# Routing of a mixture of experts, taken batch by batch into the attention of the same layer

## What is computed

```python
x = x + jnp.tanh(g_xattn[2]) * _L2_xattn_ref(_layernorm(x, axis=-1), ctx_512, ctx_512)
x = x + jnp.tanh(g_ffn[2]) * _L2_ffn_ref(_layernorm(x, axis=-1), L2_ffn_router_w, L2_ffn_w1, L2_ffn_w2)
...
logits = xf @ router_w.T
topk_vals, topk_idx = jax.lax.top_k(logits, K)
topk_w = jax.nn.softmax(topk_vals, axis=-1)
...
order = jnp.argsort(exp_id)
x_sorted = xf[order // K]
...
y1 = jax.lax.ragged_dot(x_sorted, jnp.swapaxes(w1, 1, 2), counts)
gate, up = jnp.split(y1, 2, axis=-1)
y_act = jax.nn.silu(gate) * up
y2 = jax.lax.ragged_dot(y_act, jnp.swapaxes(w2, 1, 2), counts)
...
y_pairs = y2[inv] * exp_w[:, None]
y = y_pairs.reshape(T, K, h).sum(axis=1)
```

## Time and profile before

| | us |
|---|---|
| median of 3 runs (4147.03 to 4149.95) | 4148.43 |
| the profiled execution | 4149.84 |
| its span | 4148.0 |
| TensorE busy | 3696.8 (89%) |
| VectorE busy | 1982.5 (48%) |
| ACT busy | 1365.8 (33%) |
| POOL busy | 368.5 (9%) |
| layer 2's attention, from its first score to its last addition | 1142.4 to 1643.5 |
| the tiles' loop begins | 1771.2 |

### The profile page before, as it was taken

The page is one execution under the profiler, slowest core; times in us unless marked ns, Lnnn a source line. Parts: engine busy times, 40 slices in busy tenths (PEclk is TensorE's granted clock), DMA queues, the critical chain, the costliest instruction groups (busy, mean ns, idle before and its releaser), DMA issues.

```text
span 4148.0 us, 35816 instructions
## 1 busy us (share of the span) xinstructions
PE 3696.8 (89%) x11778; PEld 1707.9 (41%) x11779; DVE 1982.5 (48%) x3525; ACT 1365.8 (33%) x2823; POOL 368.5 (9%) x387
## 2 busy tenths in 40 slices
PE   1999999966689998299969999999999998999999
PEld 0444444422344443156633444444444343444443
DVE  8646664153777774211136665656666562111111
ACT  5524341011256666022224343433434341101000
POOL 6000000000222220311110100000000000000000
PEclk6999999978889999599989999999999999999999
DMA  2322212200312330355551100000000001222221
GB/s 114 122 83 98 85 66 66 112 24 0 71 37 49 72 73 13 142 152 162 163 182 55 65 23 34 23 35 35 23 35 23 35 12 66 76 86 86 76 82 55
DMA packets 77384, 291.57 MB, mean 70 GB/s; under 512 B 10424, under 2 KB 11320, under 8 KB 66236
## 3 DMA queue, kind: packets, MB, share of 16 engines
q1 hardware_dynamic: 68928, 264.12, 19.4%
q0 software_dynamic: 8320, 25.71, 2.0%
HBM read 255.68 MB, written 33.59 MB: 70 GB/s over the span
## 4 chain that ended last, share of the span: by engine, by line
PE 78%; DVE 9%; issue 6%; ACT 4%; DMA 1%; POOL 1%; SPq 0%; DVEq 0%; ACTq 0%; POOLq 0%
PE BM L2008 6%; PE BM L2059 5%; PE BM L529 5%; PE BR L529 5%; PE BR L2067 4%; PE BM L364 4%; PE BR L364 4%; PE BS L2043 3%; PE BT L1349 3%; PE BS L545 3%; PE BT L545 3%; PE BM L2018 3%; PE BR L1694 2%; PE BM L1683 2%; PE BR L1683 2%
## 5 line engine op out<-in xcount | busy, mean ns | idle before, releaser
L2119 ACT COPY AR<-BM 128x512 f32<-128x512 f32 x340 | 199.5, 587 | 395.5 <-PE BM L2059 184.5
L2125 ACT ACTIVATE AR<-BS,AR 128x512 f32<-128x512 f32 x256 | 175.7, 690 | 410.1 <-DVE AR L2219 410.1
L2232 DVE SCALAR_TENSOR_TENSOR X<-BR,AR,X 128x512 f32<-128x512 f32 x256 | 191.9, 750 | 211.8 <-PE BR L2067 202.4
L2219 DVE TENSOR_REDUCE AR<-BS 128x2 f32<-128x1024 f32 x128 | 156.9, 1226 | 252.2 <-PE BS L2043 252.2
L2067 PE MATMUL BR<-AR 128*128 128x512 f32 x512 | 254.4, 620 | 3.9 <-DVE X L2232 0.3
L364 PE MATMUL BM<-XT,AR 128*128 (+1 forms) x512 | 233.1, 598 | 4.8 <-DMA AR<-l_w_dram 4.8
L2008 PE MATMUL BM<-XT,AR 128*128 128x512 f32 x512 | 236.6, 605 | 0.7 <-ACT XT L239 0.7
L2059 PE MATMUL BM<-AR 128*128 128x512 f32 x512 | 233.8, 599 | 0.0
L529 PE MATMUL BM<-XT,AR 128*128 128x512 f32 x512 | 230.6, 593 | 0.9 <-ACT AR L632 0.9
L529 PE MATMUL BR<-XT,AR 128*128 128x512 f32 x512 | 230.2, 592 | 0.0
L364 PE MATMUL BR<-XT,AR 128*128 (+1 forms) x512 | 230.2, 592 | 0.0
(11 more groups left out here) (335 smaller groups left out, 5945.2 us busy)
## 6 DMA issues: line engine op xcount, KB each, us to landing
AR<-l_w_dram SPq DMA_DIRECT2D x128, 512.0 KB, 3.5
AR<-l_wq_dram SPq DMA_DIRECT2D x32, 1152.0 KB, 5.1
AR<-l_w_dram SPq DMA_DIRECT2D x42, 768.0 KB, 4.7
AR<-w2h SPq DMA_DIRECT2D x16, 1024.0 KB, 4.7
QS<-qx SPq DMA_DIRECT2D x32, 512.0 KB, 9.4
AR<-l_w_dram SPq DMA_DIRECT2D x16, 1024.0 KB, 4.9
AR<-l_w_dram SPq DMA_DIRECT2D x8, 1408.0 KB, 17.2
made<-AR SPq DMA_DIRECT2D x40, 256.0 KB, 4.8
```

The costliest lines, as they stand in the source:

```text
L2119: nc.scalar.copy(to, BM[:, L3[job] % 2, :]).then_inc(m_free, 1)
L2232: nc.vector.scalar_tensor_tensor(out=xb, in0=BR[:, L3[job] % 2, :], scalar=RS3[:, p % 2, h, st:st + 1], in1=xb, op0=ALU.mult, op1=ALU.add) ...
```

## The change

Batches 0, 1 and 2 are routed while the attention of the next batch runs, and batch 3 alone at the end. With b the batch that is routed, in unit 8(b + 1) + 2 VectorE takes the statistics of the batch just finished; in the unit after it writes XN, TensorE turns it and ACT copies it once; in the next one SP stores the rows to `xnd`, TensorE makes the logits, now with the tokens as weights and the router's 8 columns moving, ACT copies them out, and VectorE chooses the experts; in the next TensorE counts and VectorE works out the places; in the last two POOL scatters, four DMAs each. The normalisation of batch 0 in units 24 and 25 is gone.

So that places are known before all tokens are counted, the table has fixed room, 2048 places for each expert, and is 128 rows of 128. At the end only the rows in use are read: VectorE works out for each partition which row its tile lies in, POOL gathers these rows with an indirect DMA, and TensorE turns them. The token numbers are therefore f32. The places in `made` (YP) are found from the fixed places by taking the room off and adding the start. At the start the table is cleared by four DMAs instead of one. The two copies of turned maxima (MTS) lie on other partitions instead of in other columns, which makes room for the routing's scratch.

```diff
-        ZERO = sb("ZERO", [P, TW], I32)
+        ZERO = sb("ZERO", [P, 32])
...
+        def routed_batch(n, k):
+            return n // KVH - 1 if n >= KVH and n % KVH == k else None
...
+        def store_rows(sp, b):
+            sp.wait_ge(xn_ready, XR[b])
+            sp.dma_start(xnd[b * S:(b + 1) * S, :].rearrange("(s p) d -> p s d", p=P), XN[:, :, :]).then_inc(xnd_in, 16)
+        def route_logits(bank, half):
+            for st in range(ST):
+                for kt in range(KT):
+                    last = nc.tensor.matmul(bank[:, st * E:(st + 1) * E], XT[:, half, kt, st * P:(st + 1) * P], RW[:, kt, :],
+                                            start=kt == 0, stop=kt == KT - 1)
+            return last
+        def route_ranks(bank):
+            n = ST * E
+            ohs = OHS.rearrange("p t e -> p (t e)")
+            nc.tensor.matmul(bank[:, 0:n], TRI, ohs, start=True, stop=True)
+            return nc.tensor.matmul(bank[:, n:2 * n], ONE, ohs, start=True, stop=True)
+        def route_top(v, b, lg):
+            for mx, of, oh in ((MX0, lg, OH0), (MX1, LG2, OH1)):
+                if oh is OH1:
+                    link(v, nc.vector.scalar_tensor_tensor(out=LG2, in0=OH0, scalar=-1.0e30, in1=lg, op0=ALU.mult, op1=ALU.add))
+                link(v, nc.vector.tensor_reduce(mx, of, op=ALU.max, axis=AX.X))
+                link(v, tt(EQ, of, one(mx, E), ALU.is_ge))
+                link(v, tt(EQ, EQ, per_e(PRIO, ST), ALU.mult))
+                link(v, nc.vector.tensor_reduce(MS, EQ, op=ALU.max, axis=AX.X))
+                link(v, tt(oh, EQ, one(MS, E), ALU.is_equal))
+            tt(OHS, OH0, OH1, ALU.add).then_inc(ohs_ready, 1)
+            link(v, tt(EX[:, b * ST:(b + 1) * ST], MX1, MX0, ALU.subtract))
+        def route_rank(v, b, ranks):
+            link(v, nc.vector.tensor_copy(PREF[:, 0, :], PREF[:, ST, :] if b else BASE))
+            for t in range(ST):
+                link(v, tt(PREF[:, t + 1, :], PREF[:, t, :], ranks[:, ST + t, :], ALU.add))
+            link(v, tt(RT[:, 0:ST, :], ranks[:, 0:ST, :], PREF[:, 0:ST, :], ALU.add))
+            for oh, idx in ((OH0, IDX0), (OH1, IDX1)):
+                link(v, tt(EQ, oh, RT[:, 0:ST, :], ALU.mult))
+                link(v, nc.vector.tensor_reduce(POS, EQ, op=ALU.add, axis=AX.X))
+                nc.vector.tensor_copy(idx[:, b * ST:(b + 1) * ST], POS).then_inc(idx_ready, 1)
+                v.wait_ge(idx_ready, 2 * b + (1 if idx is IDX0 else 2))
+        def scatter_tokens(pool, b, j):
+            pool.wait_ge(idx_ready, 2 * b + j + 1)
+            for tile in range(b * ST, (b + 1) * ST):
+                nc.gpsimd.indirect_dma_start(out=table, out_offset=bass.IndirectOffsetOnAxis(ap=(IDX0, IDX1)[j][:, tile:tile + 1], axis=0),
+                                             in_=TOK[:, tile:tile + 1], in_offset=None).then_inc(table_in, 16)
...
@@ l2_tensor @@
+                    if tt == 1 and routed_batch(n, 4) is not None:
+                        logits(routed_batch(n, 4))
+                    if tt == 1 and routed_batch(n, 5) is not None:
+                        ranks(routed_batch(n, 5))
+                    if n % KVH == 1 and tt == 3 and n // KVH < B - 1:
+                        turn_norm("n", n // KVH)
+                    if tt == 3 and routed_batch(n, 3) is not None:
+                        turn_norm("q", routed_batch(n, 3))
...
@@ l2_scalar @@
+            def take_rows(b):
+                for kt in range(KT):
+                    nc.scalar.copy(XT[:, (b + 1) % 2, kt, :], evict(("q", b, kt))).then_inc(e_free, 1)
...
@@ l2_vector @@
+                    if n % KVH == 0 and tt == 3 and b < B - 1:
+                        norm_begin(b + 1)
...
+                    if routed_batch(n, 2) is not None and tt == 3:
+                        v.wait_ge(x_done, 4 * B + b)
+                        norm_begin(b - 1)
+                    if routed_batch(n, 3) is not None and tt == 1:
+                        norm_end(b - 1, ("n", b, KT - 1) if b < B - 1 else ("q", 1, KT - 1), b - 1)
+                    if routed_batch(n, 4) is not None and tt == 3:
+                        v.wait_ge(lg_ready, b)
+                        route_top(v, b - 1, LG)
+                    if routed_batch(n, 5) is not None and tt == 3:
+                        v.wait_ge(rt_ready, b)
+                        route_rank(v, b - 1, RT)
...
@@ l2_pool, at the end of a unit @@
+                if routed_batch(n, 2) is not None:
+                    norm_pool(pool)
+                if routed_batch(n, 6) is not None:
+                    scatter_tokens(pool, routed_batch(n, 6), 0)
+                if routed_batch(n, 7) is not None:
+                    scatter_tokens(pool, routed_batch(n, 7), 1)
...
@@ moe_sync @@
+            for e in range(2):
+                up(e)
+            store_rows(sp, B - 1)
+            for e in range(2, E):
+                up(e)
...
@@ moe_tensor @@
+            norm_tensor(pe)
+            route_logits(start_job(pe, er, r), 0).then_inc(er.full, 1)
+            pe.wait_ge(ohs_ready, B)
+            route_ranks(start_job(pe, er, r)).then_inc(er.full, 1)
+            pe.wait_ge(slt_in, 16)
+            nc.tensor.transpose(start_job(pe, er, r)[:, 0:P], SLT, ID[:, :]).then_inc(er.full, 1)
...
@@ moe_vector @@
+            norm_vector(v, B - 1)
+            route_top(v, B - 1, in_tiles(full(v, er, r), ST))
+            route_rank(v, B - 1, in_tiles(full(v, er, r), 2 * ST))
...
+            nc.vector.tensor_copy(SLOTS, full(v, er, r)[:, 0:TW]).then_inc(slots_ready, 1)
...
@@ moe_pool @@
-            for tile in range(B * ST):
-                for idx in (IDX0, IDX1):
-                    nc.gpsimd.indirect_dma_start(out=table, out_offset=bass.IndirectOffsetOnAxis(ap=idx[:, tile:tile + 1], axis=0),
-                                                 in_=TOK[:, tile:tile + 1], in_offset=None).then_inc(table_in, 16)
-            pool.wait_ge(slots_in, 16)
+            for j in range(2):
+                scatter_tokens(pool, B - 1, j)
+            pool.wait_ge(row_ready, 1)
+            pool.wait_ge(table_in, 2 * B * ST * 16)
+            nc.gpsimd.indirect_dma_start(out=SLT, out_offset=None, in_=table.rearrange("(r n) o -> r (n o)", n=P),
+                                         in_offset=bass.IndirectOffsetOnAxis(ap=ROW, axis=0)).then_inc(slt_in, 16)
+            pool.wait_ge(slots_ready, 1)
```

More of the change, by code:

```diff
@@ L1642, in moe_tensor @@
             pe.wait_ge(x_done, 5 * B)
[L1643 to L1649, removed]
[L1650 to L1660 removed]
+            norm_tensor(pe)
+            pe.wait_ge(turn.free, T_PE.now() + 2)
+            route_logits(start_job(pe, er, r), 0).then_inc(er.full, 1)
[3 more added lines that the diff above has]
+            nc.tensor.transpose(start_job(pe, er, r)[:, 0:P], SLT, ID[:, :]).then_inc(er.full, 1)
             pe.wait_ge(turn.free, T_PE.now() + 2)
@@ L1710, in moe_scalar @@
                 act.sem_inc(q.free, 2)
-            for b in range(B):
-                nc.scalar.copy(LT[0:E, :], full(act, em, m)[0:E, :]).then_inc(em.free, 1)
-                if b < B - 1:
-                    norm_scalar(act, (b + 1) & 1)
+            norm_scalar(act, 0)
             act.wait_ge(pair_exp_in, 1)
@@ L1751, in moe_vector @@
                 v.sem_inc(y_stored[u], 16)
-            v.wait_ge(router_in, 64)
-            nc.vector.memset(ONE, 1.0).then_inc(ones_ready, 1)
-            for b in range(B):
-                bank = full(v, er, r)
-                nc.vector.tensor_copy(LG[:, b * ST:(b + 1) * ST, :], bank[:, 0:ST * E].rearrange("p (s e) -> p s e", e=E)).then_inc(er.free, 1)
-                if b < B - 1:
-                    v.wait_ge(xnd_in, 16 * (b + 1))
-                    norm_vector(v, b + 1)
-                    T_V.step(KT)
@@ L1782, in moe_vector @@
-            bank = full(v, er, r)[:, 0:n128].rearrange("p (t e) -> p t e", e=E)
-            nc.vector.tensor_copy(TOTAL, bank)
-            nc.vector.tensor_copy(SCAN0, bank).then_inc(er.free, 1)
-            v.wait_ge(er.free, r.now() + 2)
+            v.wait_ge(x_done, 5 * B)
+            v.wait_ge(e_full, L2["q", B - 2, KT - 1] + 1)
+            v.wait_ge(xnd_in, 16 * (B - 1))
+            norm_vector(v, B - 1)
+            T_V.step(KT)
+            in_tiles = lambda bank, n: bank[:, 0:n * E].rearrange("p (t e) -> p t e", e=E)
@@ L2317, in _ @@
             sp.wait_ge(zero_ready, 1)
-            sp.dma_start(table.rearrange("(p n) o -> p (n o)", p=P), ZERO[:, :]).then_inc(table_zero, 16)
+            for c in range(4):
+                sp.dma_start(table.rearrange("(p n) o -> p (n o)", p=P)[:, 32 * c:32 * c + 32], ZERO[:, :]).then_inc(table_zero, 16)
             l0_sync(sp)
```

225 lines of the change are left out of this document (127 added, 98 removed).

## The result

The changed kernel takes 4126.67 us (median of four executions, 4124.98 to 4127.68), the kernel before 4148.76 us beside it: ratio 0.9947, 95% interval 0.9932 to 0.9962. It is faster by 22 us, where 48 were forecast, and lies just above the range (4084 to 4126). The span of its profiled execution is 4124.4 us.

The account below looks back on a forecast made before the run. TensorE, busy 89%, gains only where it stands still: the 127.7 us serial chain after layer 2's attention. End -81.9 us plus attention +33.8 us gives -48.1 us, so 4100 us, range 4084 to 4126.

Parts of the forecast that it names:

- The first gather of tokens: End stage: gathering the first tile's tokens before its transpose takes 5.5 us, bounds 3.5 and 6.5.
- lands 2.13 us later: End stage: the eighth scatter of batch 3 lands 2.13 us after its start, at 1678.6 us.
- only the last one counts, and it starts after the load has ended: End stage: up-weight load ends at 1672 us, so slow scatter landings beside it do not matter.
- the maxima behind the scatters: Attention: storing a batch's rows on SP's queue costs nothing, since the next maxima come 14 us later.
- router product and choosing: Attention, units 12, 20 and 28: router product 4.5 us and choosing 2.0 us for each batch.
- 3.1: Attention, unit after the statistics: normalising and transposing costs 3.1 us per batch, bounds 1.9 and 6.0.
- Scatters on POOL: nothing: Attention, ends of units 14/15, 22/23, 30/31: eight scatters per batch cost nothing at 1.27 us each.
- the slow rival: POOL and VectorE hold each other up in attention; gain gone at 4.7 us a scatter, 4180 us at 6; chance 0.04.
- behind 24: Attention, units 24/25: batch 0's normalising is no longer done there, saving 7.65 us.
- the clock's fall: Rival: VectorE blocks drop TensorE's clock in attention, which pays 60 us; total 4126 us; chance 0.15.
- the end gains less: Rival: table reads and scatters late behind expert weights; end gains 74.5 us instead of 81.9; 4108 us; chance 0.10.
- three signs of being wrong: Attention: router product much over 5 us, scatters over 1.3 us, or units behind 24 not losing 7.6 us.

Follow-up runs that it names:

- the whole version: Changed kernel with tokens written 512 bytes apart, table read by one plain load ahead of the down loads, routed batches' normalising one step later: 4102.31 us, ratio 0.9876.
- the run that moved it: Changed kernel with a routed batch's normalising moved one pair of score blocks later in units 11, 19 and 27: 4123.55 us, ratio 0.9933.
- places apart alone: Changed kernel with scatters writing consecutive tokens of an expert 512 bytes apart, table read unchanged and so misread: 4110.20 us, kernel before 4152.62 us.
- folded places: Changed kernel with table places folded so eight consecutive tokens of an expert lie 64 bytes or more apart: 4114.25 us, ratio 0.9908.

## Why the prediction went wrong

The gain was forecast as 81.9 us at the end less 33.8 in attention; the end gave 64.6, and attention paid 43.4.

**What held.** TensorE's standstill at the end was the place to gain, and most of that chain came out as built from the rows of before (forecast and measured): normalising 6.4 and 7.0, transposes and copies 4.4 and 4.4, router product 7.0 and 7.0 at a clock of 0.50, choosing 2.9 and 2.7, ranks with the steps to the first index and POOL's start 3.3 and 3.2, scatters at 1.27 and 1.30 us each, table gather 3.5 and 3.9 with its start. The first gather of tokens was too dear, 5.5 against 3.5.

**What failed at the end** is one step: "lands 2.13 us later", taken from the earlier trace rows, with "only the last one counts, and it starts after the load has ended". The scatters' pitch was carried over rightly, their landing was not: it depends on the addresses, and the change of the table's layout, which the section on the change describes, was never priced. 20.26 - 2.13 = 18.1 us; less the 2.0 us of the first gather, plus 1.0 us of small terms (normalising 0.6, the table's gather 0.4), that is the 17.1 us by which 46 was exceeded. The second half of the step failed too. The up load had not ended: its last packet came 43.9 us after attention's end, against 33.8 with places 512 bytes apart, so the slow writes held it up. And even where it had ended, the two down loads, which the forecast itself let leave early and counted only for the gather, ran beside the last scatter: 5.7 us there, 2.1 in the whole version, where they leave behind the table.

**What failed in attention** is the size of one term, normalising, and a term put at nothing, the maxima behind the scatters. Measured as each step's sum over all batches above plain units of 13.95 us (the last batch's ranks above 12.31, their stretch before):

| step | forecast | measured |
|---|---|---|
| statistics | 6.0 | 4.4 |
| normalising and transposing | 9.3 | 15.8 |
| router product and choosing | 19.5 | 20.9 |
| ranks | 6.6 | 3.6 |
| batch 0's old normalising gone | -7.65 | -7.5 |
| late maxima behind scatters (before units 16 and 24) | 0 | 7.8 |
| first units and clock, not of the change | 0 | -1.7 |
| sum | 33.8 | 43.3 |

"3.1" for normalising was wrong in its size: it subtracted four ACT copies from stretches in which VectorE's pass took 3.2 us or less, and did not look at what POOL does in units 11 and 19. By the run that moved it, and by unit 27, the step costs 1.9 us without POOL, the low end that the prediction gave. "Scatters on POOL: nothing" was right for POOL, and the slow rival (scatters that take over 2.7 us on POOL) did not come: in attention they took 0.95 to 1.12 us. It overlooked that the maxima's writes, issued behind the scatters, count as landed only among the scatters' landings. The Trainium skill, "DMA: Bandwidth & Descriptors", section "Queues, rings and completion order", says that the count which ends a transfer lands only after every earlier write of the same DMA engine, across its queues. The trace agrees: the rows of the maxima were moved by 1413.8 us and counted at 1421.9, and with places 512 bytes apart, where the scatters end at once, they were moved by 1418.3 and counted at 1418.7. The "behind 24" units lost their 7.5 us as said.

**The rivals.** The measured 4127 us is next to the 4126 of the clock's fall, but not by that cause: attention paid 43, not 60. The router product took 3.9 us in unit 12, 3.7 in unit 20 and 4.3 in unit 28, near the lower of its bounds of 3.5 and 7.0: the granted clock of these stretches was 0.92, 0.92 and 0.85, but it fell in the last third of the product or behind it. Of "the end gains less" the mechanism was partly there, but the end gained 64.6 us, less than its 74.5, and loads count for only 2.5 to 3.5 of the 18.1 us by which the last landing was late. None of the three signs of being wrong came (the product at most 4.3 us, a scatter at most 1.12 us on POOL, the units behind 24 cheaper by 7.5), so they would not have found the fault. With places apart alone the end stage is 49.4 us. With the pass moved as well and the down loads behind a plain load of the table (the whole version) it is 45.6 us, forecast 46; attention there takes 1676.0 - 1162.8 = 513.2 us, forecast 480.0 + 33.8 = 513.8, though partly by errors that cancel (the stretch of router product and choosing is 21.9 us in it).

The prediction had no row for the router product at full clock; unit 20 has one, its 32 passes starting (3.5 / 31 =) 0.113 us apart at a granted clock of 1.00:

```profile
L1260 PE MATMUL BS<-AR,XT x32: 256/256/277, 1504.5 to 1508.0; 128*128 128x8 f32 x32
```

The Trainium skill, "TensorE: Matmul & The Clock Gate", section "LDWEIGHTS (loading the stationary operand)", prices a weight load at columns / 1.2 ns, by which an estimate for 128 columns is 0.107 us; the trace agrees. So the router product itself was 0.2 to 0.8 us cheaper than the 4.5 assumed, and what surrounds it dearer: 8.9 us in the three batches instead of 6.0.

## What to carry to other kernels

A scattered write has two prices, the issue and the landing; the second goes by the addresses, so when a table's layout changes, price it anew, and keep small writes that are in flight together apart (64 bytes were enough here). Whatever else goes through the same DMA engines, a tiny transfer that gates the next unit too, lands behind such writes. And a price taken from a stretch holds only with the neighbours it had there: look up what POOL does beside each moved VectorE pass.

## What the hardware showed that was not expected

- Writes of 4 bytes to places 4 bytes apart in DRAM land late, those 64 or 512 bytes apart do not; by that the first wait for each other. Where between 4 and 64 bytes the limit lies, and what waits, no run shows. With no load beside, eight scatters whose packets had all gone out by 1724.3 us landed until 1740.2; spread over the eight that is (1740.2 - 1715.4) / 8 = 3.1 us a scatter, or, at 16 neighbours of an expert in each, some 0.2 us a write (an estimate from these times). At 64 bytes batch 0's landings end 0.4 us behind their last packets.
- While that goes on, the DMA engines can count as busy (1.24 of a window) at 43 GB/s, and two 8 KB writes of the maxima that were long moved count as landed 8 us late.
- Why batch 0's scatters trailed by 6.5 and 8.6 us even with folded places (the first four: last packet 1418.8, last landing 1425.3), and those of batches 1 and 2 by 1 to 2, was not settled.
